# Decoder on one core: expert weights of the last feed-forward kept in SBUF, batch 1's experts in two halves of 256 tokens

## The reference, cut to what matters

```python
# layer 1, cross-attention: 16 heads of 8, 77 context rows
scores = einsum('bhsd,bhnd->bhsn', Q, K) / sqrt(8)
topk_scores, topk_indices = top_k(scores, 32)
sparse_weights = softmax(topk_scores)
context = einsum('bhsk,bhskd->bhsd', sparse_weights, take(V, topk_indices))
x = x + context @ Wo.T + bo
# layer 1, feed-forward: every token goes through all 8 experts
xt = layernorm(x)                                   # 1024 tokens x 128
scores = softmax(xt @ Wr.T)
k_scores, k_ids = top_k(scores, 2)
combine = sum(one_hot(k_ids, 8) * (k_scores / (k_scores.sum() + eps)), axis=1)
g = einsum('td,efd->etf', xt, Wg)                   # Wg, Wu: 8 x 512 x 128
u = einsum('td,efd->etf', xt, Wu)
out_e = einsum('etf,edf->etd', relu(g) * u, Wd)     # Wd: 8 x 128 x 512
x = x + einsum('te,etd->td', combine, out_e)
```

## Time and profile before

| | |
|---|---|
| median of 3 runs | 686.44 us (686.42 to 686.87) |
| profiled execution | 685.04 us |
| its span in the profile | 683.3 us |
| granted PE clock, mean | 0.924 of full speed |
| PE busy | 577.8 us, 85% |
| DVE busy | 429.2 us, 63% |
| first up of batch 0 | starts at 445.09 us |
| first up of batch 1 | starts at 584.50 us |

### The profile page before, as it was taken

How to read it: one execution, slowest core, us unless ns; L and a number is a source line. 1 busy time by engine, 2 the same in 40 slices (tenths; PEclk the granted TensorE clock), 3 DMA queues, 4 the chain that set the end, 5 groups by cost and what they waited for, 6 DMA issues and landing times.

```text
span 683.3 us, 11976 instructions
## 1 busy us (share of the span) xinstructions
PE 577.8 (85%) x3975; PEld 461.5 (68%) x3975; DVE 429.2 (63%) x2325; ACT 308.0 (45%) x725; POOL 225.4 (33%) x208
## 2 busy tenths in 40 slices
PE   5875469987898889899987887799999998889997
PEld 3644259984665556776665565678888776678886
DVE  3754877623434688766757778649999994243333
ACT  2321123225764675657534556334545443324442
POOL 3001410002333365545443456254444443211220
PEclk9965579999999999999989999979999999789999
DMA  5100003211200000000000000301112121013210
GB/s 155 37 0 0 2 0 94 63 35 42 71 1 1 1 1 2 1 1 2 1 1 1 0 2 1 94 1 48 47 53 78 40 64 47 0 48 93 70 40 15
DMA packets 32186, 21.46 MB, mean 31 GB/s; under 512 B 1840, under 2 KB 28924, under 8 KB 32125
## 3 DMA queue, kind: packets, MB, share of 16 engines
q1 hardware_dynamic: 32125, 20.70, 10.2%
HBM read 20.17 MB, written 0.52 MB: 30 GB/s over the span
## 4 chain that ended last, share of the span: by engine, by line
PE 58%; DVE 25%; ACT 11%; issue 4%; POOL 1%; DMA 0%; DVEq 0%; ACTq 0%; POOLq 0%
PE ps L1512 49%; DVE wk L1022 5%; DVE top L1012 4%; DVE nmax L958 4%; ACT w_mem L1324 3%; PE ps L2021 2%; ACT cat_mem L1308 2%; PE ps L1840 2%; DVE cat_mem L1137 2%; ACT pr L1324 1%; DVE hits L856 1%; PE ps L1902 1%; PE ps L1742 1%; DVE x L1148 1%; DVE xn L985 1%
## 5 line engine op out<-in xcount | busy, mean ns | idle before, releaser
L1512 PE MATMUL ps<-cat_mem 128*128 128x128 f32 (+6 forms) x784 | 127.7, 354 | 17.4 <-DVE cat_mem L1137 10.1
L1512 PEld LDWEIGHTS ps<-cat_mem 128*128 128x128 f32 (+1 forms) x784 | 86.9, 196 | 38.6 <-DVE cat_mem L1137 16.2
L1137 DVE TENSOR_TENSOR cat_mem<-gr,ps 128x512 f32<-128x512 f32 x64 | 43.8, 686 | 80.1 <-ACT gr L1458 78.5
L958 DVE TENSOR_REDUCE nmax<-ps 128x2 f32<-128x256 f32 (+1 forms) x64 | 51.2, 820 | 57.1 <-PE ps L1512 57.1
L1022 DVE MATCH_REPLACE8 wk<-top,wk 128x77 f32<-128x77 f32 x384 | 80.6, 224 | 0.0
L582 POOL TENSOR_TENSOR w_mem<-w_mem,rinv 128x256 f32<-128x256 f32 (+3 forms) x44 | 53.1, 1219 | 82.0 <-DVE rinv L964 81.7
L648 POOL TENSOR_TENSOR w_lo<-cat_mem,w_hi 128x512 fp32r<-128x512 f32 x32 | 40.9, 1283 | 79.6 <-ACT w_hi L1444 79.6
L1512 PE MATMUL ps<-x_hi,w_hi 128*128 128x512 f32 x128 | 60.0, 468 | 2.3 <-issue 1.2
L1441 ACT ACTIVATE cat_mem<-ps 128x512 f32<-128x512 f32 x48 | 28.6, 596 | 65.2 <-PE ps L2021 65.1
L1012 DVE MAX8 top<-wk 128x8 f32<-128x77 f32 x384 | 57.9, 223 | 0.0
L1512 PE MATMUL ps<-x_hi,w_lo 128*128 128x512 f32 x128 | 53.0, 414 | 0.0
(11 more groups left out here) (267 smaller groups left out, 1236.2 us busy)
## 6 DMA issues: line engine op xcount, KB each, us to landing
w_mem<-in_L_ffn_W_dram SPq DMA_DIRECT2D x16, 256.0 KB, 3.0
fn<-in_L_ffn_Wg_dram SPq DMA_DIRECT2D x8, 256.0 KB, 2.8
fn<-in_L_ffn_Wu_dram SPq DMA_DIRECT2D x8, 256.0 KB, 3.5
fn<-in_L_ffn_Wd_dram SPq DMA_DIRECT2D x8, 256.0 KB, 3.7
cat_mem<-in_L_ffn_Wg_dram SPq DMA_DIRECT2D x8, 256.0 KB, 2.9
cat_mem<-in_L_ffn_Wu_dram SPq DMA_DIRECT2D x8, 256.0 KB, 3.3
cat_mem<-in_L_ffn_Wd_dram SPq DMA_DIRECT2D x8, 256.0 KB, 3.8
x<-in_x_dram SPq DMA_DIRECT2D x2, 256.0 KB, 3.3
```

Of the source, the lines that this page charges most:

```text
L958: dve.tensor_reduce(nmax[:, i % 8, :], ps[:, 2 * s:2 * s + 2, at:at + (c + 1) * P], X, ALU.max, negate=True).then_inc(nmax_ready, 1)
L1137: dve.tensor_tensor(hg[s][:, :], gr[s][:, :], ps[:, 2 * s + 1, :], ALU.mult)\
L1512: return pe.matmul(dst, lhsT, rhs, start=start, stop=stop, skip_group_check=shared)
```

## The change

All weights of the eight experts are prepared once and stay: w_hi[8] and w_lo[8] (4 KB of each partition an expert) and fd[8], the transposed Wd (2 KB). They lie where tensors of the stages before lay, which are now allocated in a scope that is closed (`early.close()`) before the late tensors are allocated. `turn_f`, `evac_f`, `weights_lo` and the loads run for m = 0 to 7 only. hg moves to sel_mem, fT keeps only Wg and Wu.

Batch 1 is cut in block 2 and block 3. A step f = 32 to 63 has two chunks of 128 hidden features on 256 tokens, so that the two PSUM banks of a step are full again: twelve fp32r matmuls with 256 columns instead of six with 512; relu and gate as before (128x512), four down matmuls as before. An expert has two steps for each half: f = 32 to 47 are the eight experts on block 2, 48 to 63 the same on block 3. A combine has two instructions there instead of four.

The pieces of the top-32 are dealt out by the table FEED: units 9 to 11 at 12 of the steps 0 to 15 (none where f % 4 is 3), units 12 and 13 at every second step of 16 to 30, units 14 and 15 at every step 32 to 39; PE's and POOL's work behind unit 15 stands at steps 40 to 42. Block 2's context, norm and router stand at steps 21 to 27, block 3's at 43 to 48. up(48) is the only one that isn't issued a step ahead: it follows down(47) and norm_two(3).

```diff
+def expert_of(f):
+    return divmod(f, FC) if f < FC * E else (E + (f - FC * E) // 2, f % 2)
+FEED = {f: 36 + k for k, f in enumerate([f for f in range(16) if f % 4 < 3] + [16, 18, 20, 22, 24, 26, 28, 30]
+                                        + list(range(32, 43)))}
+def piece_in(f):
+    return divmod(FEED[f], 4) if f in FEED else (None, None)
...
+        early.close()
+        w_hi += [sb(f"w_hi{e}", [P, 2, FC, P], f32r) for e in range(2, E)]
+        w_lo += [sb(f"w_lo{e}", [P, 2, FC, P], f32r) for e in range(2, E)]
+        fd = [sb(f"fd{e}", [P, FC, P]) for e in range(E)]
...
-            for m in range(2, 2 * E):
+            for m in range(2, E):
                 sp.wait_ge(fT_ps, 3 * (m - 1))
-                load_f1(m % E, m % 2)
+                load_f1(m, m % 2)
...
-            for m in range(E - 1):
-                n = 9 + m
-                if m == 5:
+            for f in range(FC * E + 2 * E):
+                n, r = piece_in(f)
+                m, c = expert_of(f)
+                if f == 24:
                     rstd_two(2, gn_var, gn_rstd)
-                gone(n - 1)
-                pick(n - 1)
-                if m == 0:
+                if f == 46:
+                    rstd_two(3, gn_var, gn_rstd)
+                if r == 0:
+                    gone(n - 1)
+                    pick(n - 1)
+                if f == 1:
                     add_bo(3)
-                shift(n)
-                weights_lo(m + 1)
-            gone(15)
-            pick(15)
-            weights_lo(E)
...
+                if r == 1 and n < 16:
+                    shift(n)
+                if m < E - 1 and c in (1, 2):
+                    weights_lo(m + 1, c - 1)
...
+            def up(f):
+                m, c = expert_of(f)
+                s, e = f % 2, m % E
+                pe.wait_ge(w_lo_ready, 2 * e + 2)
+                if f >= 2:
+                    pe.wait_ge(hg_ready, f - 1)
+                if f < FC * E:
+                    i, parts, n, high, low_part = 0, ((c, 0),), S, x_hi[0][:, :], x_lo[0][:, :]
+                else:
+                    i, n = m // E, 2 * P
+                    parts = ((2 * c, 0), (2 * c + 1, n))
+                    high, low_part = x_hi[1][:, n * (i - 1):n * i], x_lo[1][:, n * (i - 1):n * i]
+                for k in range(2):
+                    for cc, at in parts:
+                        mm(ps[:, 2 * s + k, at:at + n], w_hi[e][:, k, cc, :], high, start=at == 0, stop=False, shared=True)
+                        mm(ps[:, 2 * s + k, at:at + n], w_lo[e][:, k, cc, :], high, start=False, stop=False, shared=True)
...
+            for f in range(FC * E + 4 * E):
+                n, r = piece_in(f)
+                m, c = expert_of(f)
+                if f + 1 < FC * E + 4 * E and f != 47:
+                    up(f + 1)
...
+                down(f)
...
+                if f == 47:
+                    four = norm_two(3, gn_ready, gnT_ps, gnT_ready, out_x, *four)
+                    pe.wait_ge(x_hi_ready, 3)
+                    up(48)
+                    route(3, 6, 2, 4, *four)
```

522 lines of the change are left out of this document (253 added, 269 removed).

## The result

The changed kernel takes 675.17 us (median of 4 runs, 673.45 to 675.99), the kernel before beside it 686.63 (4 runs, 686.42 to 686.87). The ratio is 0.983, 95% interval 0.9808 to 0.9851. The forecast was 663.3 with a range of 655 to 674: the sign was right, the size was not, and the time lies outside the range. The profiled execution took 675.76 us, its span is 674.0.

What follows compares the result with a forecast made beforehand. DVE was taken to bound batch 0 and PE batch 1. down(31) at 563.0, then 33.0, 19.7, 41.1 and 3.4 us gave a span of 660.2; plus 1.7 and 1.4 this made 663.3 us, range 655 to 674.

Steps and rivals of the forecast that it cites:

- The bound before: Before the change: DVE sets batch 0's pace by less than 1 us an expert; PE alone sets batch 1's, 10.55 us.
- the sum from step 32 on: Steps 32 to 39 set by DVE, 33.0 us; then PE, 19.7 to down(47); seam at 48 through PE's last matmul 41.1.
- The price of the 256-column matmul: Batch 1's up: an fp32r matmul with 256 columns taken at 0.118 us, near the downs' 0.115; a step 2.34 us.
- rival B: Steps 32 to 63: 256-column matmuls don't overlap their loads, 0.225 us each, time 696; decides from 0.18 on; chance 0.05.
- Steps 0 to 3. As before up to down(3): The stretch ahead of the top-32's closer packing: unchanged, down(3) starts at 468.08 us as in the trace before.
- In all 6.1: Steps 3 to 31: PE's stalls total 6.1 us, on top of 88.8 us of PE work, making 94.9.
- Both waits: PE's stalls for POOL's w_lo at up(8) and up(12), where masks stand ahead: 1.4 and 2.4 us.
- 2.3 us more: Steps 3 to 31: PE's stalls in the other steps, behind the contexts, from chaining gate, piece, combine and relu: 2.3 us.
- The rule for this: Steps 3 to 31: a step with piece and combine needs 4.7 us of DVE against PE's 3 to 4.6.
- my sum: PE's work from down(3) to down(31), steps, transposes, top-32 and block 2's small matmuls: 88.8 us.
- Rival A: PE's clock falls in thinned steps 32 to 39, and at the seam and w_lo stalls: 668 to 676 us; chance 0.18.
- 12 transposes, 1.32 us, 8 experts: 10.6 us, all on the chain: Batch 1: twelve PE transposes per expert removed, all 10.6 us lying on the chain.

Runs made afterwards that it cites:

- Experiments 1 and 2: 1: changed kernel again unedited, 673.86 us, and with one DVE memset of 1536 columns near its start, 674.77; 2: kernel before, unedited, profiled again, 685.58.
- the changed kernel's repeat: The changed kernel run again with nothing edited, for a second trace: 673.86 us, ratio 0.9827 to the kernel before.
- experiment 3: Changed kernel with POOL's subtraction for w_lo ahead of the top-32's mask and shift in each step: 669.62 us, ratio 0.976.
- experiment 5: On top of experiment 3, top-32 pieces moved to steps without a combine, block 2's chain one step later: 667.33 us, ratio 0.975.
- experiment 7: Changed kernel with three unread 128x128 transposes added on PE in each of batch 1's 32 steps: 678.11 us, ratio 0.9883.
- the second kernel of experiment 9: Changed kernel with only block 1's router gates moved to step 0: 672.05 us, ratio 0.9815. (The first made that move in experiment 6's kernel: 662.06, 0.9697.).
- experiments 5 and 6: 6: experiment 3's POOL order, pieces in three of four steps through 1 to 31, up(48) issued a step ahead: 666.47 us, 0.9739. (5: own line.).
- experiment 8: Experiment 6's kernel with the first top-32 piece in step 2, not 1, and block 3's chain from step 40: 666.71 us, ratio 0.9736.
- experiment 4: Changed kernel with a top-32 piece in every step of batch 0, blocks 2 and 3's chains earlier, up(48) a step ahead: 672.50 us, ratio 0.9809.

## Why the prediction was right and wrong

**The bound before, and the sum from step 32 on: right.** Steps 32 to 40 are DVE's (30.81 of 32.6 us busy) and took 32.6 for 33.0. A step of batch 1 is 2.32 for 2.34, the seam with all behind it 41.1 for 41.1, and its parts fit too: up(48) starts 1.30 us after the norm's transposes for 1.3, the wait for the router is 1.08 for 1.2, the last down waits 0.52 for the 0.5. (Before the change DVE set batch 0's pace by 15.4 - 14.3 = 1.1 us an expert, not by "less than 1" as I wrote; nothing hangs on it.)

**The price of the 256-column matmul: right.** 0.117 us for the 0.118; rival B is out. What decided for it, eight pairs of load and matmul at 0.115, carried over to fp32r. (The 0.18 us from which B was to decide left out the 8 us that it hides in steps 32 to 39; with them it is 0.118 + 31.1 / 384 = 0.20.)

**The first step that failed is "Steps 0 to 3. As before up to down(3)".** No instruction moved there, and yet down(3) came 4.8 us later. Experiments 1 and 2: the level of the clock in 425 to 447 us differs between executions of one kernel, up(0) lies from 445.1 to 451.3 in the thirteen traces, and the kernel before does this too, at 445.1 and 449.3. Its two traces end 0.3 us apart because one loses between the batches what the other loses at 430. I had read the 0.78 of the earlier trace rows as a property of the place between the batches, and taken the 445.09 as fixed without a look at the clock ahead of it; in these two traces an early fall went with a smaller one later. The error is 4.8 us of the 13.8. About 3 of it stand between the two traces of before as well; the rest is how late this one execution was, since the changed kernel's repeat had gate(3) 1.7 us earlier.

**The second is the term of the stalls in steps 3 to 31, "In all 6.1".** The stretch was to shrink from 109.2 to 94.9 us and took 103.6: PE was idle 10.0 us for the 6.1 and busy 93.6 for 88.8. Of the 8.6 us that were missing, experiment 3 gives 4.5 back, of which 3.0 are the waits for w_lo and about 1.5 the clock behind them. Both waits were foreseen, at 3.8; the lower clock behind one of them was not in the term. The waits for gate were 5.9 us where "2.3 us more" stood for all others. In experiment 5, where no step has both a combine and a piece on DVE, they fell by 3.8, with a time gain of 1.7 us over that stretch and the next. The rule for this was in my text (4.7 us of DVE against 3 to 4.6 of PE), but I let the empty step behind it pay that back, which it does for DVE and not for PE. With both w_lo waits gone PE is still busy 92.0 us in experiment 3 at a clock of 1.00, 3.2 more than my sum; no run here assigns these.

**Rival A had a part of the mechanism, in the wrong place.** The clock stayed at 1.00 in steps 32 to 39, where PE was thinned, with waits up to 1.1 us. It fell around single long waits elsewhere. Behind up(0) the thirteen traces have 15 waits of PE over 2 us. Twelve of them had the lower level begin inside them or within 1.3 us of their end: 2.08 or 2.09 us (the changed kernel in both its traces and with the memset, experiment 7, and the second kernel of experiment 9), 3.1 (experiments 5 and 6), 3.6 (experiment 8), 4.4 (experiment 4), and in the kernel before 3.06 twice and 2.70. Three, of 2.13, 2.69 and 2.94 us, were not followed by it. Nor does every fall need such a wait: in the first trace of before (at 464), in experiment 3 (467) and in experiment 7 (464) the clock fell with no wait of 1 us or more since up(0). So the length of one wait makes a fall likely and doesn't decide it; what does is open. That the measured 675.2 us lies in A's 668 to 676 is chance, since A's price stood in steps 32 to 39, at the seam and at the stalls, and only the stall at up(12) had it.

**"12 transposes, 1.32 us, 8 experts: 10.6 us, all on the chain" was too high as a saving.** Put back into the changed kernel they cost 5.6 us by the gates, and 3.6 to 3.8 by the ratios of the medians. The forecast itself went by steps and didn't use the 10.6, so nothing of the error comes from it.

**From the profiled execution to the median** I added 1.4 us; here the median was 0.6 under the profiled one. This took 2.0 us off the error: 13.8 - 2.0 = 11.9 us between 663.3 and 675.2, with rounding.

**The range** was too narrow for what it left out: that the same code reaches up(0) anywhere from 445 to 451 us was in none of its cases, nor was a fall of the clock behind a stall for w_lo outside rival A, and neither was a longer row of waits for gate.

What stays open: why the clock falls in 425 to 447 us earlier in one execution than in another, why it fell behind some waits over 2 us and not behind others, and the 3.2 us of PE's busy time. The memset of experiment 1 says nothing of the first, since its delay was gone long before 425 us.

## What to carry to other kernels

When a part of a trace with a low clock is removed, look where the same execution had its clock high, and take a second profile of the unchanged kernel before calling the difference a gain. When a resource is packed closer, let the range hold slow matmuls behind each wait of PE over 2 us (twelve of 15 had them here), and place short chains (a router, a norm) where their engine is idle, before looking at which work they follow: here the same work in another order made the gain nearly twice as large, 3.0% for 1.7%. An uneven engine is not evened out by an idle step behind a full one if another engine waits in the full one.
